# One-core Trainium2 kernel of a six-block perceiver: an entry by batch to the experts, a spread cross attention, and moved ternary pieces

## The reference, cut to what matters

```python
x = x + xattn0(ln(x), ctx)      # 32 heads of 8, q and k rms-normed per head, softmax over 2048 keys
x = x + attn0(ln(x))            # 16 heads of 128, causal, softmax over 128 keys
x = x + ffn0(ln(x))             # silu(x w1') * (x w3') then w2'; w' = weights quantised to -1, 0, 1 times a scale
x = x + xattn1(ln(x), ctx)      # s_t = sigmoid(decay) s_(t-1) + W_in ctx_t; mean of W_out s_t; layer norm
x = x + attn1(ln(x))            # convolution, cos/sin phases, cumulative sums, gated output
x = x + moe(ln(x))              # see below

def moe(x):                     # 16 experts of 176, 4 chosen per row, and a shared one of 704
    p = softmax(x @ gate_w.T);  w, idx = top_k(p, 4);  w = w / w.sum()
    shared = down(silu(x g) * (x u)) * sigmoid(x @ shared_gate_vec.T)
    return shared + sum_e w_e * down_e(silu(x g_e) * (x u_e))
```

## Time and profile before

| | us |
|---|---|
| median of three runs | 418.57 (418.25 to 418.73) |
| the profiled execution | 418.47 |
| its span, first to last instruction | 416.7 |
| PE, DVE, ACT, POOL busy | 390.9, 303.2, 264.6, 208.4 |
| mean granted TensorE clock | 0.992 |

### The profile page before, as it was taken

How to read it: one execution, slowest core, us unless ns; L and a number is a source line. 1 busy time by engine, 2 the same in 40 slices (tenths; PEclk the granted TensorE clock), 3 DMA queues, 4 the chain that set the end, 5 groups by cost and what they waited for, 6 DMA issues and landing times.

```text
span 416.7 us, 14345 instructions
## 1 busy us (share of the span) xinstructions
PE 390.9 (94%) x6017; PEld 326.3 (78%) x6017; DVE 303.2 (73%) x687; ACT 264.6 (64%) x543; POOL 208.4 (50%) x259
## 2 busy tenths in 40 slices
PE   6979999999999999889999999999889998999997
PEld 4656667777667777669999897878778887989995
DVE  6788989997888887767999976778997658222220
ACT  3457878888888888976544543724999235544441
POOL 2468757765567775105654430610598536445530
PEclk8989999999999999999999999999999999999999
DMA  4097651542321100280000017210000670000000
GB/s 161 6 336 223 206 165 49 180 129 75 96 78 42 31 28 3 105 327 4 2 2 1 2 43 304 63 78 1 1 2 3 238 324 0 2 2 2 0 2 25
DMA packets 10833, 34.78 MB, mean 83 GB/s; under 512 B 2193, under 2 KB 7313, under 8 KB 8977
## 3 DMA queue, kind: packets, MB, share of 16 engines
q1 hardware_dynamic: 10480, 33.08, 23.2%
q10 hardware_dynamic: 288, 0.79, 0.5%
HBM read 33.60 MB, written 0.26 MB: 81 GB/s over the span
## 4 chain that ended last, share of the span: by engine, by line
PE 62%; DVE 22%; POOL 6%; issue 5%; ACT 3%; DMA 1%; SPq 0%; DVEq 0%; POOLq 0%; ACTq 0%
PE ps L1748 10%; PE ps L1225 8%; PE ps L1703 8%; PE ps L1211 6%; PE ps L1735 4%; PE ps L1718 3%; PE ps L953 3%; PE ps L935 2%; PE ps L451 2%; PE ps L894 2%; PE ps L901 2%; PE ps L512 2%; PE ps L1199 1%; DVE sb_big L1454 1%; PE ps L381 1%
## 5 line engine op out<-in xcount | busy, mean ns | idle before, releaser
L1669 ACT ACTIVATE sb_arena<-ps 128x1024 f32<-128x1024 f32 x128 | 123.4, 1019 | 22.2 <-PE ps L1735 21.5
L1748 PE MATMUL ps<-sb_arena 128*25 128x128 f32 (+1 forms) x2048 | 69.0, 274 | 0.3 <-ACT sb_arena L1669 0.3
L1748 PEld LDWEIGHTS ps<-sb_arena 128*25 128x25 f32 (+1 forms) x2048 | 50.4, 97 | 7.6 <-ACT sb_arena L1669 0.7
L1703 PE MATMUL ps<-sb_halves 128*128 128x512 f32 x192 | 54.4, 419 | 1.7 <-DVE sb_arena L1473 1.0
L1257 POOL TENSOR_TENSOR sb_halves<-sb_big,sb_halves 128x704 fp32r<-128x704 f32 x20 | 33.7, 1689 | 38.7 <-ACT sb_halves L1251 38.7
L1323 DVE SCALAR_TENSOR_TENSOR sb_arena<-ps,sb_w_q,sb_arena 128x176 f32<-128x176 f32 x40 | 15.9, 401 | 42.7 <-ACT sb_arena L1275 42.5
L1703 PEld LDWEIGHTS ps<-sb_halves 128*128 128x128 f32 x192 | 34.5, 192 | 14.4 <-issue 6.2
L1225 PE MATMUL ps<-sb_halves 128*128 128x352 f32 x240 | 42.9, 332 | 2.0 <-POOL sb_halves L1257 2.0
L1563 POOL TENSOR_TENSOR sb_big<-sb_arena 128x256 f32<-128x256 f32 x31 | 19.0, 614 | 49.2 <-DVE sb_arena L1434 49.2
L541 POOL TENSOR_TENSOR sb_halves<-sb_big,sb_halves 128x256 fp32r<-128x256 f32 x28 | 21.0, 771 | 43.9 <-ACT sb_halves L525 43.9
L1225 PEld LDWEIGHTS ps<-sb_halves 128*128 128x128 f32 x240 | 39.1, 189 | 3.3 <-DVE sb_arena L1323 1.7
(11 more groups left out here) (240 smaller groups left out, 848.3 us busy)
## 6 DMA issues: line engine op xcount, KB each, us to landing
sb_arena<-in_ctx SPq DMA_DIRECT2D x32, 128.0 KB, 2.4
sb_mid<-in_w_down SPq DMA_DIRECT2D x1, 3584.0 KB, 12.6
sb_big<-in_w_gu SPq DMA_DIRECT2D x1, 3520.0 KB, 11.9
sb_mid<-in_w_ffn SPq DMA_DIRECT2D x3, 768.0 KB, 4.4
sb_big<-in_w_gu SPq DMA_DIRECT2D x1, 2112.0 KB, 7.6
sb_big<-in_w_q SPq DMA_DIRECT2D x2, 1024.0 KB, 6.2
sb_big<-in_w_k SPq DMA_DIRECT2D x2, 1024.0 KB, 5.8
sb_big<-in_w_v SPq DMA_DIRECT2D x2, 1024.0 KB, 5.9
```

The source lines that it names most:

```text
L1669: nc.scalar.activation(probs[:, n % P_SLOTS].rearrange("p a g n -> p a (g n)"), ps[:, bank:bank + 2], ACT.Exp, scale=XD ** -0.5).then_inc( ...
L1703: i = T.matmul(ps[:, 7], ctx_half[:, t % 2, c, kt], wkv_half[:, d, kt], start=(n + kt == 0), stop=(n == 2 and kt == KT - 1))
L1748: i = T.matmul(ps[32 * gg:32 * gg + m, 6, j * P:(j + 1) * P], v_sb[:, t % V_SLOTS, 4 * gg + j, head], probs[:, n % P_SLOTS, a, gg], start= ...
```

## The change

It has four parts.

1. **Cross attention, entry.** `x` gets its own semaphore, so the layer norm no longer waits for `id32`; `w_xkv` and `w_xq` go from ACT's queue to SP's behind `id32`, the decay's transfer goes the other way. The first two `take_k` and the first values (tiles 1 to 4) are done by ACT instead of DVE; DVE does the decay rate ahead of the copy of the turned layer norm, and the first two scans ahead of the query norm.
2. **Cross attention, loop.** `pack_q1` is cut into five operations at t = 7 to 11, behind `weigh_context`; the q norm's small operations move to t = 4 and 6; the second batch's queries are turned at t = 13 into a score bank and copied out by ACT; ACT copies the first batch's sums at t = 16 in one operation; the sum of weights is done in 16 pieces of 128 columns, at t = 14 to 29, ahead of `mean_squares`.
3. **Self-attention.** Ternary pieces: before the mask at i = 6, 8, 10, 12 and now 14; at the end at i = 4, 7, 8, 9, 11, 12, 13 instead of 4, 6, 8, 9, 10, 11, 12, 14.
4. **End of phase and experts.** `sum_y` finishes batch 0 before it does batch 1's last two parts. Layer norm, turning and splitting go batch by batch; the bridge shrinks from 24 products to 6; the routing comes behind the first unit's first products; unit 2 is split by DVE.

```diff
-            sp.dma_start(id32[:], io["id32"]).then_inc(sem("x_loaded"), 16)
+            sp.dma_start(id32[:], io["id32"]).then_inc(sem("id32_loaded"), 16)
+            sp.dma_start(w_xkv, io["w_xkv"]).then_inc(sem("wkv_loaded"), 16)
+            sp.dma_start(w_xq, io["w_xq"]).then_inc(sem("wq_loaded"), 16)
...
-            dve.wait_ge(sem("x_loaded"), 32)
+            dve.wait_ge(sem("x_loaded"), 16)
             layer_norm(dve, LN_OF["xattn"])
-            ln_copy(dve, 0, 0)
...
             for t in range(NB):
                 if t + 2 < NB:
                     take_k(t + 2)
-                    take_v(t + 2)
+                    if t + 2 not in ACT_VALUES:
+                        take_v(t + 2)
                     if t + 2 < MB:
                         decay_weights(t + 2)
+                    else:
+                        sum_weights(t + 2 - MB)
                     mean_squares(t + 2)
-                if t == 6:
-                    take_q(1)
...
-                if t == MB:
-                    take_acc(0)
...
-                if MB <= t < MB + 4:
...
-                    V.tensor_reduce(gsums[:, n:n + 1], geo[:, n * 512:(n + 1) * 512], AX_X, ALU.add
...
                 weigh_context(t)
-                if t == 4:
-                    pack_q1()
+                if t == TURN_AT - 6:
+                    norm_q1()
+                if TURN_AT - 5 <= t < TURN_AT - 3:
+                    high_q1(t - TURN_AT + 5)
+                if TURN_AT - 3 <= t < TURN_AT - 1:
+                    low_q1(t - TURN_AT + 3)
...
                     exps(SUBS * t + c)
+                    if c == 0 and t + 2 in ACT_VALUES:
+                        first_values(t + 2)
...
+                    if t == TURN_AT and c == 2:
+                        turned_queries(1, 2 * ((SUBS * t + 1) % 3))
+                    if t == MB and c == 0:
+                        act.wait_ge(sem("pv_done"), SUBS * MB)
+                        nc.scalar.copy(accs[:, 0], ps[:, 6]).then_inc(sem("acc_taken"), 2)
...
-                if i in (6, 8, 10, 12):
+                if i in (6, 8, 10, 12, 14):
                     ternary(*next(pieces))
...
-                if i in (4, 6, 8, 9, 10, 11, 12, 14):
+                if i in (4, 7, 8, 9, 11, 12, 13):
                     ternary(*next(pieces))
...
-            sum_y(1)
-            sum_y(2)
+            sum_y(1, 0)
+            sum_y(2, 0)
+            sum_y(1, 1)
+            sum_y(2, 1)
...
-        WARM = {0: 20, 1: 14, 2: 19, 5: 58, 6: 24}
+        WARM = {0: 20, 1: 14, 2: 19, 5: 58, 6: 6}
...
+                if b == 0 and u == 2:
+                    pe.wait_ge(sem("third_low"), 1)
...
+            dve.wait_ge(sem("gu_projected"), B)
+            V.tensor_copy(gu_half[:, 0, 0], unit_weights(2)).then_inc(sem("third_high"), 1)
+            dve.wait_ge(sem("third_high"), 1)
+            V.tensor_tensor(gu_half[:, 0, 1], unit_weights(2), gu_half[:, 0, 0].bitcast(F32), ALU.subtract
+                            ).then_inc(sem("third_low"), 1)
```

More of the change, by code:

```diff
@@ L50 @@
 ROUND_MAGIC = 1.5 * 2.0 ** 23
+ACT_VALUES = (1, 2, 3, 4)
+TURN_AT = 13
 LATE_GU = slice(4 * 2 * EI, E * 2 * EI)
@@ L958, in tensor_phase, with sum_y @@
                     turn_y(0)
-            def sum_y(t):
+            def sum_y(t, b):
                 pe.wait_ge(sem("yT_taken"), t + 1)
-                for b in range(B):
-                    for u in range(2 * t, 2 * t + 2):
-                        i = T.matmul(ps[:, 3 + b, 0:D], yT[:, u, b * P:b * P + P], w_out2[:, u], start=(u == 0), stop=(u == 5))
-                    if t == 2:
-                        i.then_inc(sem("phase_out"), 1)
+                for u in range(2 * t, 2 * t + 2):
+                    i = T.matmul(ps[:, 3 + b, 0:D], yT[:, u, b * P:b * P + P], w_out2[:, u], start=(u == 0), stop=(u == 5))
+                if t == 2:
+                    i.then_inc(sem("phase_out"), 1)
             pe.wait_ge(sem("y_gated"), 3 * B)
@@ L971, in tensor_phase @@
             pe.wait_ge(sem("y_scaled"), 3 * B)
-            sum_y(0)
+            for b in range(B):
+                sum_y(0, b)
             pe.wait_ge(sem("last_y_gated"), B)
@@ L1179, in tensor_experts, with turn_x, route @@
             T = nc.tensor
-            ln_transpose(pe, LN_OF["moe"], 0)
-            pe.wait_ge(sem("xnT_ready"), 4)
-            pe.wait_ge(sem("w_moe"), loaded["w_moe"])
-            for b in range(B):
+            keep_warm(WARM[LN_OF["moe"]], 0)
+            def turn_x(b):
+                pe.wait_ge(sem("ln_normed"), B * LN_OF["summary2"] + b + 1)
+                for kt in range(KT):
+                    i = T.transpose(ps[:, 6 * b, kt * P:(kt + 1) * P], xn[:, b, kt * P:(kt + 1) * P], id32[:])
+                i.then_inc(sem("ln_transposed"), 1)
+            def route(b):
+                pe.wait_ge(sem("xnT_ready"), 4 + b)
+                pe.wait_ge(sem("w_moe"), loaded["w_moe"])
                 for kt in range(KT):
@@ L1227, in tensor_experts @@
                 i.then_inc(sem("gu_projected"), 1)
+                if k == 0:
+                    for b in range(B):
+                        route(b)
+                    b = 0
                 if b == B - 1:
@@ L1301, in vector_experts, with stats, aggregate, normalise @@
             V = nc.vector
-            layer_norm(dve, LN_OF["moe"], add_previous)
-            ln_copy(dve, 5, 0)
-            split_x(dve, xe_half, 0, "xe")
-            dve.wait_ge(sem("routed"), 1)
+            def stats(b):
+                add_previous(b)
+                step(dve, V.bn_stats(bn[:, b], x[:, b]))
+            def aggregate(b):
+                V.bn_aggr(mv[:, b], bn[:, b]).then_inc(sem("ln_stats"), 1)
+            def normalise(b):
+                dve.wait_ge(sem("ln_rstd"), B * LN_OF["moe"] + b + 1)
+                V.tensor_scalar(xn[:, b], x[:, b], mv[:, b, 0:1], rstd[:, b:b + 1], ALU.subtract, ALU.mult
+                                ).then_inc(sem("ln_normed"), 1)
+            def turned(b):
+                return ps[:, 6 * b, 0:256].rearrange("p (k l) -> p k l", k=KT)
+            def high(b):
+                dve.wait_ge(sem("ln_transposed"), 8 + b)
+                V.tensor_copy(xe_half[:, 0, :, b * P:b * P + P], turned(b)).then_inc(sem("xe_high"), 1)
+            def low(b):
+                dve.wait_ge(sem("xe_high"), b + 1)
+                V.tensor_tensor(xe_half[:, 1, :, b * P:b * P + P], turned(b), xe_half[:, 0, :, b * P:b * P + P].bitcast(F32),
+                                ALU.subtract).then_inc(sem("xe_low"), 1)
+            def whole(b):
+                V.tensor_copy(xnT[:, :, b, 3:], turned(b)).then_inc(sem("xnT_ready"), 1)
+            stats(0)
+            aggregate(0)
+            normalise(0)
+            stats(1)
+            aggregate(1)
+            high(0)
+            low(0)
+            normalise(1)
+            whole(0)
+            high(1)
+            whole(1)
+            low(1)
+            dve.wait_ge(sem("routed"), B)
             V.tensor_copy(lg, ps[:, 1, 0:64].rearrange("p (b n) -> p b n", b=B)[:, :, 0:17]).then_inc(sem("logits_taken"), 1)
@@ L1696, in project @@
                     pe.wait_ge(sem("kv_taken"), t)
+                    pe.wait_ge(sem("k_taken"), t)
                 if t >= 3:
```

157 lines of the change are left out of this document (83 added, 74 removed).

## The result

The changed kernel takes 416.22 us (median of 13 executions, 415.01 to 418.0) against 418.73 beside it: a ratio of 0.9939, 95% interval 0.9927 to 0.9952. The forecast was 412.2, in a range of 408.8 to 415.8. The direction was right, the size was not: 2.5 us came of 6.4. The profiled execution took 415.42 us, at a granted clock of 1.000; 7 of the 13 executions had a mean clock of 0.992 to 0.996 and took 417.0 on average, the other six 415.9; only the profiled one, at full clock, has a trace.

What follows compares the result with a forecast made beforehand. PE was taken as the bound, busy 390.9 of 416.7 us, leaving its idle time and low clock to gain. Cross attention -4.35, self-attention -0.1 and experts -1.9 sum to -6.35: 412.2 us by the median, range 408.8 to 415.8.

Steps and rivals of the forecast that it cites:

- Entry, -4.0: Cross attention up to the second tile's scores: no wait for the identity, no half clock, 4.0 us less.
- the chain to the first scores: Cross attention's entry: DVE's and ACT's norms and packing become PE's wait; first scores 1.4 us earlier, from 18.90 to 17.5.
- Tiles 1 to 7, -1.2: Cross attention, tiles 1 to 7: ACT's value copies cost 1.2 us, the removed lumps give more back; from -4.0 to -5.2.
- The lumps of t=4 and t=6: Cross attention: POOL's lump at t=4 goes, 1.2 us less, and the turning at t=6 goes, 1.5 us less.
- Tiles 7 to 16, +2.05: Cross attention's loop: five POOL operations beside DVE cost 1.4 us, the turning at t=13 costs 0.65.
- Tiles 16 to 30, -1.2: Cross attention's loop: four long sums go, -2.2 us; sixteen short sums cost 0.3, ACT's copy of the first batch's sums 0.7.
- Self-attention, -0.1: Self-attention: moved ternary pieces shorten PE's waits for normed probabilities by 0.1 us net, bounds -0.8 and +0.6.
- the reading of the waits: Self-attention: freeing places at i = 6 and 10 gains about 0.3 us each; the piece at i = 7 costs 0.5.
- Experts, -1.9: Experts' entry: earlier first products and unit 2 split on DVE avoid waits for POOL, 1.9 us less, bounds -0.3 and -2.3.
- The rival of the falling clock: Experts' entry: with six bridging products the clock falls to half, costing 1.5 us, total 413.7; chance 0.10.
- The rival of dear sums: Tiles 14 to 29: each short sum costs 0.55 us like a long one, 8.8 in all, total 420.7; chance 0.06.
- that of ACT and POOL as the new bound: Cross attention: POOL extras cost 2.85 us instead of 1.4, ACT's copies at t = 13 and 16 1.35 more; 415.0; chance 0.12.

Runs made afterwards that it cites:

- three of the kernels above: The changed kernel with POOL's query operations one tile later (416.12 us), values of tiles 2 to 4 on DVE (415.78), or ten more bridging products ahead of `project(0)` (418.10).
- four profiles of kernels with the same short bridge: The changed kernel with 512-column sums (417.33 us), old ternary places (416.20), values of tiles 2 to 4 on DVE (415.78), or ten more entry bridging products (418.10).
- the best kernel: The changed kernel with weighings late, query operations later, first batch's sums and values on DVE, old ternary places, five more bridging products: 412.00 us, ratio 0.9818.

## Why the prediction was wrong, point by point

Forecast and measured sum are 3.45 us apart: 1.34 of it lies in the last tiles and the self-attention, 1.10 in the entry, 0.73 in tiles 16 to 30 and 0.35 in tiles 1 to 7.

- **Entry, -4.0, measured -2.90.** The mechanism was right: the first statistics start at 3.77 us, and both low clocks are gone in the profile. From the first to the second tile's scores 2.82 us were gained (2.6 was said). The step that failed is the chain to the first scores, put at 17.5 and measured at 18.82: it has no cost for POOL beside DVE there, though the prediction priced just that, 0.98 against 0.41, two parts later. The change's early weighings stretch DVE's query packing; without them the first scores come at 17.62. The low clock is not gone for good: three of the kernels above show it at 19 to 23 us, and their first tile then takes 7.3 to 7.6 us instead of 6.1.
- **Tiles 1 to 7, -1.2, measured -0.85.** `first_values` cost 0.7 a tile where 0.6 was said. The lumps of t=4 and t=6 went as said, but the step that failed is that the moved query norm was given no cost before tile 7. It stands in POOL's list ahead of the next tile's squares and waits for ACT: 1.1 us.
- **Tiles 7 to 16, +2.05, measured +1.87.** Near in size by luck: 0.55 of it is a stall of PE's stream, which the prediction does not have, so that the five operations and the turning cost 1.32, not 2.05.
- **Tiles 16 to 30, -1.2, measured -0.47.** The sums were right in kind: the short ones cost nothing from tile 22 on (0.3 was said, 0.29 us of DVE each, measured 0.28), and tiles 17 to 20 fell, but by 1.59 instead of 2.2. ACT's copy was right: 5.82 against 5.08 is 0.74 (+0.7). What is missing are 0.61 in tiles 17 to 20 and 0.37 in tile 21. Stalls of 0.16 and 0.32 us stand in tiles 19 and 21, and those tiles take 0.43 and 0.37 more than a plain one. The profile puts the second stall down to exponentials, but the other profiles speak for the stalls: in five of them tile 21 has one at the same instruction, of 0.19 to 0.86 us, and takes 4.97 to 5.63 us; in the nine without it takes 4.70 to 4.81. No run was made for this alone.
- **Self-attention, -0.1, measured +0.84**, outside its bound of +0.6. The step that failed is the reading of the waits: the places freed at 6 and 10 gave nothing, where 0.6 was said, the one at 7 took 0.68 (0.5 was said), and 0.34 came behind the start of step 15, where the prediction has no term for the pieces put at 13 and 14. The old places give all 0.84 back. The other 0.40 of the table's +1.24 lies in the last tile, where a stall of 1.11 us (shown above) took the place of a wait of 0.70 before:

```profile
175.99 0.64 PE L1735 MATMUL ps<-sb_w_ri,sb_arena 32*128 32x128 f16 x16 [0.70 <-ACT sb_arena L1669]
```
- **Experts, -1.9, measured -1.79** in this execution, and by the mechanism that was said: unit 2's two operations on DVE take 0.53 and 0.89 us (0.6 and 0.9), and k=4 does not wait for POOL. Two times of that sum are 0.3 to 0.4 above what their parts add up to (343.9 for 343.5, 344.4 for 344.1), less than tells here. The rival of the falling clock, given one chance in ten, came true in four profiles of kernels with the same short bridge, at 1.2 to 1.3 us where 1.5 was said. The changed kernel's median is 0.8 above its profiled execution, and 7 of its 13 executions have a low clock; whether they lost it here or in the entry is not recorded.

The rival of dear sums is refuted; that of ACT and POOL as the new bound was nearest, with 415.0, but its reason did not hold: the POOL operations of tiles 7 to 16 and ACT's copy at t = 16 cost no more than said. With the misses mended the same design takes 412.00, near the forecast of 412.2; part of that closeness is chance, since the forecast held the costs of `first_values` and of ACT's copy, which the best kernel avoids, and it has stalls in its stream.

## What to carry to other kernels

Before a step is moved onto an engine that waits in order, look what stands behind it there: a small operation that waits for another engine's late result holds everything behind it. Here 0.63 us of work waited 2.39 us and cost PE 1.1. Spreading work into a real wait was free (reductions of 0.28 us, each in a wait of 0.33, cost nothing), but moving it beside another engine was not (0.97 us instead of 0.43), and in the entry this was missed. When PE's bridge of idle products is shortened, look at the clock of several executions, not of one.
